# Row LSTM: forget and input gate by one activation over two banks, new values written into moved lanes, each row stored by itself

## What is computed

```python
def _L3_conv_ref(X, W_is, b_is, W_ss, b_ss):
    ...
    its = lax.conv_general_dilated(X, W_is * mask, ..., padding=((0, 0), (1, 1))) + b_is
    def step(carry, row_in):
        h, c = carry
        ss = lax.conv_general_dilated(h, W_ss, ..., padding=((1, 1),)) + b_ss
        g5 = (ss + row_in).reshape(B, 3, 4, Oc, Wd)
        f = jax.nn.sigmoid(g5[:, :, 0].reshape(B, O, Wd))
        i = jax.nn.sigmoid(g5[:, :, 1].reshape(B, O, Wd))
        o = jax.nn.sigmoid(g5[:, :, 2].reshape(B, O, Wd))
        g = jnp.tanh(g5[:, :, 3].reshape(B, O, Wd))
        c_new = f * c + i * g
        h_new = o * jnp.tanh(c_new)
        return ((h_new, c_new), h_new)
    _, hs = lax.scan(step, (h0, c0), xs)      # over the 56 rows
```

## Time and profile before

| | |
|---|---|
| runs | 3912.57, 3913.15, 3914.15 us; median 3913.15 |
| the profiled execution | 3912.36 us, of which the span of the trace is 3910.5 |
| busy over the span | PE 82%, PEld 46%, DVE 70%, ACT 67%, POOL 42% |
| the row LSTM, first matmul to the barrier behind it | 3344.1 to 3718.2 us |

### The profile page before, as it was taken

How to read it: one execution, slowest core, us unless ns; L and a number is a source line. 1 busy time by engine, 2 the same in 40 slices (tenths; PEclk the granted TensorE clock), 3 DMA queues, 4 the chain that set the end, 5 groups by cost and what they waited for, 6 DMA issues and landing times. The chain is left out here.

```text
span 3910.5 us, 70731 instructions
## 1 busy us (share of the span) xinstructions
PE 3205.9 (82%) x20680; PEld 1815.2 (46%) x20680; DVE 2733.1 (70%) x4347; ACT 2623.9 (67%) x4852; POOL 1638.0 (42%) x1502
## 2 busy tenths in 40 slices
PE   5799999978678898999999666878888678677666
PEld 2688888844224343444444222433343334566522
DVE  2566666657319998999999992749999867122256
ACT  4455555559698888989889434966666378465556
POOL 0233333310147888989889761007677600000000
PEclk9899999989889999999999997989999889798988
DMA  4100000012365747576674522210000022400022
GB/s 95 28 14 14 14 14 14 14 32 60 86 165 161 193 134 197 141 209 172 175 204 120 135 58 68 59 36 20 21 21 20 12 50 54 87 13 13 17 56 51
DMA packets 209512, 297.93 MB, mean 76 GB/s; under 512 B 73866, under 2 KB 193854, under 8 KB 208962
## 3 DMA queue, kind: packets, MB, share of 16 engines
q1 hardware_dynamic: 198546, 285.75, 28.2%
q10 hardware_dynamic: 10800, 10.34, 1.1%
HBM read 193.87 MB, written 102.03 MB: 76 GB/s over the span
## 5 line engine op out<-in xcount | busy, mean ns | idle before, releaser
L1586 POOL TENSOR_TENSOR mam_hc<-mam_h,mam_cs 128x896 f32<-128x896 f32 x336 | 704.0, 2096 | 181.4 <-DVE mam_h L1551 93.3
L1551 DVE TENSOR_TENSOR_SCAN mam_h<-mam_a,mam_kept,mam_dbx 128x448 f32<-128x448 f32 x672 | 737.5, 1127 | 19.9 <-ACT mam_a L1437 18.5
L1318 PE MATMUL mam_ps_y<-mam_hc,mam_ident 128*128 128x448 f32 x1344 | 569.7, 557 | 132.5 <-POOL mam_hc L1586 132.2
L1987 POOL TENSOR_TENSOR scan_ch<-scan_h,scan_cs 128x392 f32<-128x392 f32 x256 | 342.6, 1357 | 394.4 <-DVE scan_h L1931 317.3
L1437 ACT ACTIVATE mam_a<-mam_ft,mam_a_neg 128x448 f32<-128x448 f32 x672 | 409.3, 657 | 79.5 <-DVE mam_h L1551 78.7
L1318 PEld LDWEIGHTS mam_ps_y<-mam_hc,mam_ident 128*128 128x128 f32 x1344 | 248.5, 192 | 431.8 <-POOL mam_hc L1586 222.7
L1538 DVE TENSOR_TENSOR mam_dbx<-mam_ps_u,mam_bs 128x448 f32<-128x448 f32 x672 | 380.8, 610 | 34.2 <-DMA mam_bs<-dram_bc 34.2
L766 POOL TENSOR_TENSOR att_prob<-att_prob,att_share 128x588 f32<-128x588 f32 x128 | 151.6, 1184 | 452.5 <-DVE att_share L951 452.5
L2107 PE MATMUL lstm_ps<-lstm_hs,lstm_w_h 64*128 64x224 f32 x1344 | 175.8, 417 | 97.0 <-DVE lstm_hs L2190 97.0
L418 PE MATMUL f_xc_ff<-all_x,f_centre 128*128 (+1 forms) x256 | 127.8, 583 | 138.8 <-DVE all_x L308 138.7
L886 ACT ACTIVATE att_pt<-att_ps_t 128x512 f32<-128x512 f32 x128 | 76.4, 597 | 210.2 <-PE att_ps_t L827 210.2
(11 more groups left out here) (214 smaller groups left out, 7464.4 us busy)
## 6 DMA issues: line engine op xcount, KB each, us to landing
mam_taps<-normed SPq DMA_DIRECT2D x1008, 43.5 KB
mam_bs<-dram_bc SPq DMA_DIRECT2D x28, 896.0 KB, 14.3
mam_cs<-dram_bc SPq DMA_DIRECT2D x28, 896.0 KB, 16.6
mam_ft<-dram_steps SPq DMA_DIRECT2D x42, 448.0 KB, 4.8
normed<-f_staged SPq DMA_DIRECT2D x384, 38.1 KB
f_mixed<-mixed SPq DMA_DIRECT2D x384, 36.8 KB
dram_gs<-mam_gs SPq DMA_DIRECT2D x56, 224.0 KB, 2.1
mam_gt<-dram_gs SPq DMA_DIRECT2D x56, 224.0 KB, 2.7
```

Of the source, the lines that this page charges most:

```text
L1318: mm = pe.matmul(ps_y[p % 2][:, 0:MT], ident[:], hc[t % 2][:, i, :], start=False, stop=(t % 8 == 7 and i == 1))
L1551: dve.tensor_tensor_scan(h[:, n % 8, :], a[t % 3][:, i, :], dbx[:, i, 0:MT], kept[:, at:at + 1], ALU.mult, ALU.add).then_inc(scanned, 1)
L1586: pool.tensor_tensor(hc[t % 2][:], h[:, row:row + 2, :], cs[:, 2 * pair:2 * pair + 2, :], ALU.mult).then_inc(weighed, 1)
L1987: pool.tensor_tensor(out, hd, in_order(cs, 1 - half, d, k), ALU.mult).then_inc(weighed, 1)
```

## The change

- The pairs are made anew: pair 0 is forget and input gate, pair 1 new values and output gate.
- The biases of pair 0 are added on TensorE: one more matmul per half in `from_input`, of `w_bias` (two rows of each half hold the two bias vectors) with a tile of ones. So both gates of both halves go through one Sigmoid without bias, 128 lanes by 2 banks by 224, into `opened`.
- The Tanh of the new values comes behind the second pair's sum; it writes each half into the other half's lanes, so that it lies beside its input gate. Each half counts up `tanhed`.
- The output gate stays two activations, into a tile of its own.
- VectorE's products of forget and input gate are done by halves: kept[half] = opened x cell in the same lanes, as soon as `opened` is there; added[half] = opened x new, read in the other half's lanes and written to this one's, as each Tanh is done. Kept comes before added.
- Each row is stored as it comes, by 4 DMAs of 24 channels by 4 images by 56 values (`store_row`), all on SP but for the last row, of which ScalarE issues two.
- SP loads `w_bias` (64 KB) ahead of the first input rows, and VectorE sets the ones.

```diff
@@ -2009,13 +2009,16 @@
         buf = Buffers(nc, ctx, "lstm")
         w_x = buf.sbuf("w_x", [P, 2, PAIRED, P])
         w_h = buf.sbuf("w_h", [P, 3, PAIRED, P])
-        biases = buf.sbuf("biases", [P, 2, GATES])
-        bias = buf.sbuf("bias", [P, GATES])
+        biases = buf.sbuf("biases", [P, 2, 2])
+        bias = buf.sbuf("bias", [P, 2])
+        w_bias = buf.sbuf("w_bias", [P, P])
+        ones = buf.sbuf("ones", [P, J * SIDE])
         xs = buf.sbuf("xs", [P, J, PAD, PAD])
         hs = buf.sbuf("hs", [P, J, SIDE + 1, PAD])
         cell = buf.sbuf("cell", [P, J, SIDE])
         new = [buf.sbuf(f"new{p}", [P, J, SIDE]) for p in range(2)]
-        gates = [buf.sbuf(f"gates{p}", [P, 3, J, SIDE]) for p in range(2)]
+        opened = [buf.sbuf(f"opened{p}", [P, 2, J, SIDE]) for p in range(2)]
+        output = [buf.sbuf(f"output{p}", [P, J, SIDE]) for p in range(2)]
         kept = [buf.sbuf(f"kept{p}", [P, J, SIDE]) for p in range(2)]
         added = [buf.sbuf(f"added{p}", [P, J, SIDE]) for p in range(2)]
         squashed = [buf.sbuf(f"squashed{p}", [P, J, SIDE]) for p in range(2)]
@@ -2025,12 +2028,12 @@
                                  "zeroed", "stored",
                                  "stored_last"))
         rows_in = [buf.sem(f"rows_in{part}") for part in range(len(LOADED))]
-        summed, tanhed, inputs, forgets, outputs, kepts, addeds, cells, squasheds, hidden = (
-            buf.sem(n) for n in ("summed", "tanhed", "inputs", "forgets", "outputs", "kepts",
-                                 "addeds", "cells", "squasheds", "hidden"))
+        summed, opens, tanhed, outputs, kepts, addeds, cells, squasheds, hidden = (
+            buf.sem(n) for n in ("summed", "opens", "tanhed", "outputs", "kepts", "addeds",
+                                 "cells", "squasheds", "hidden"))
         W = J * SIDE
-        NEW_INPUT, FORGET_OUTPUT = 0, 1
-        FORGET, INPUT, OUTPUT = 0, 1, 2
+        FORGET_INPUT, NEW_OUTPUT = 0, 1
+        NEW, OUTPUT = 0, 1
         LANES = (slice(0, HALF_LANES), slice(HALF_LANES, P))
 
         def each_row(eng, row):
@@ -2059,45 +2062,56 @@
             eng.dma_start(xs[lane + C:lane + 32, J - 1, first:end, :].rearrange(
                 "c y q -> c (y q)"), normed[0, 0:32 - C, at]).then_inc(rows_in[part], 16)
 
-        def store_rows(eng, g, k, done):
-            for j in range(J):
-                eng.dma_start(mixed[k + (j * G + g) * K].rearrange("c (r q) -> c r q", q=SIDE),
-                              group_rows(hs, g)[:, j, bass.ds(k * ROWS + 1, ROWS), 1:SIDE + 1]
-                              ).then_inc(done, 16)
+        by_group = mixed.rearrange("(j g k) c n -> g k c j n", g=G, k=K)
+
+        def store_row(eng, g, k, r, done):
+            eng.dma_start(by_group[g, k][:, :, r * SIDE:(r + 1) * SIDE],
+                          group_rows(hs, g)[:, :, bass.ds(k * ROWS + (r + 1), 1), 1:SIDE + 1
+                                            ].rearrange("c j o q -> c j (o q)")
+                          ).then_inc(done, 16)
 
         with nc.Block() as block:
             @block.sync
             def _(sp):
                 sp.dma_start(w_x[:], w["rl_w_x"]).then_inc(x_weights_in, 16)
+                sp.dma_start(w_bias[:], w["rl_w_bias"]).then_inc(x_weights_in, 16)
                 load_rows(sp, 0)
                 sp.dma_start(biases[:], w["rl_b"]).then_inc(biases_in, 16)
                 load_rows(sp, 1)
                 load_rows(sp, 2)
                 with sp.Fori(0, K - 1) as k:
-                    sp.wait_ge(hidden, k * ROWS + ROWS)
+                    for r in range(ROWS):
+                        sp.wait_ge(hidden, k * ROWS + (r + 1))
+                        for g in range(G):
+                            store_row(sp, g, k, r, stored)
+                for r in range(ROWS - 1):
+                    sp.wait_ge(hidden, (K - 1) * ROWS + r + 1)
                     for g in range(G):
-                        store_rows(sp, g, k, stored)
+                        store_row(sp, g, K - 1, r, stored)
                 sp.wait_ge(hidden, SIDE)
                 for g in range(0, G, 2):
-                    store_rows(sp, g, K - 1, stored_last)
-                sp.wait_ge(stored, 16 * IMAGES * (K - 1))
-                sp.wait_ge(stored_last, 16 * IMAGES)
+                    store_row(sp, g, K - 1, ROWS - 1, stored_last)
+                sp.wait_ge(stored, 16 * G * (SIDE - 1))
+                sp.wait_ge(stored_last, 16 * G)
 
             @block.tensor
             def _(pe):
                 pe.wait_ge(zeroed, 1)
-                pe.wait_ge(x_weights_in, 16)
+                pe.wait_ge(x_weights_in, 32)
                 pe.wait_ge(rows_in[0], 16 * (G + 2))
 
                 def from_input(y, p):
 
                     reached(pe, outputs, y - 1)
+                    for half, lanes in enumerate(LANES):
+                        pe.matmul(ps[p][:, FORGET_INPUT, half, 0:W], w_bias[lanes, :],
+                                  ones[lanes, :], start=True, stop=False)
                     for pair in range(PAIRED):
                         for tap in range(2):
                             for half, lanes in enumerate(LANES):
                                 pe.matmul(ps[p][:, pair, half, 0:W], w_x[lanes, tap, pair, :],
                                           xs[lanes, :, y + 1, tap:tap + SIDE],
-                                          start=(tap == 0), stop=False)
+                                          start=(pair == NEW_OUTPUT and tap == 0), stop=False)
 
                 def row(y, p):
                     reached(pe, hidden, y)
@@ -2128,42 +2142,35 @@
                 def row(y, p):
                     act.wait_ge(summed, y * PAIRED + 1)
                     reached(act, cells, y)
-                    for half, lanes in enumerate(LANES):
-                        act.activation(new[p][lanes].rearrange("c j q -> c (j q)"),
-                                       ps[p][lanes, NEW_INPUT, half, 0:W], ACT.Tanh,
-                                       bias=bias[lanes, 0:1])
-                    for half, lanes in enumerate(LANES):
-                        other = LANES[1 - half]
-                        mm = act.activation(gates[p][lanes, INPUT].rearrange("c j q -> c (j q)"),
-                                            ps[p][other, NEW_INPUT, half, 0:W], ACT.Sigmoid,
-                                            bias=bias[other, 1 + INPUT:2 + INPUT])
-                    mm.then_inc(inputs, 1)
+                    act.activation(opened[p][:].rearrange("c h j q -> c h (j q)"),
+                                   ps[p][:, FORGET_INPUT, :, 0:W], ACT.Sigmoid
+                                   ).then_inc(opens, 1)
                     act.wait_ge(summed, y * PAIRED + 2)
                     reached(act, hidden, y)
                     for half, lanes in enumerate(LANES):
-                        mm = act.activation(gates[p][lanes, FORGET].rearrange("c j q -> c (j q)"),
-                                            ps[p][lanes, FORGET_OUTPUT, half, 0:W], ACT.Sigmoid,
-                                            bias=bias[lanes, 1 + FORGET:2 + FORGET])
-                    mm.then_inc(forgets, 1)
+                        act.activation(new[p][LANES[1 - half]].rearrange("c j q -> c (j q)"),
+                                       ps[p][lanes, NEW_OUTPUT, half, 0:W], ACT.Tanh,
+                                       bias=bias[lanes, NEW:NEW + 1]).then_inc(tanhed, 1)
                     for half, lanes in enumerate(LANES):
                         other = LANES[1 - half]
-                        mm = act.activation(gates[p][lanes, OUTPUT].rearrange("c j q -> c (j q)"),
-                                            ps[p][other, FORGET_OUTPUT, half, 0:W], ACT.Sigmoid,
-                                            bias=bias[other, 1 + OUTPUT:2 + OUTPUT])
-                    mm.then_inc(outputs, 1)
+                        op = act.activation(output[p][lanes].rearrange("c j q -> c (j q)"),
+                                            ps[p][other, NEW_OUTPUT, half, 0:W], ACT.Sigmoid,
+                                            bias=bias[other, OUTPUT:OUTPUT + 1])
+                    op.then_inc(outputs, 1)
                     act.wait_ge(cells, y + 1)
                     act.activation(squashed[p][:], cell[:], ACT.Tanh).then_inc(squasheds, 1)
 
                 each_row(act, row)
                 act.wait_ge(hidden, SIDE)
                 for g in range(1, G, 2):
-                    store_rows(act, g, K - 1, stored_last)
+                    store_row(act, g, K - 1, ROWS - 1, stored_last)
 
             @block.vector
             def _(dve):
 
                 dve.memset(hs[:, :, 0, :], 0.0)
                 dve.memset(hs[:, :, 1:, 0:PAD:PAD - 1], 0.0)
+                dve.memset(ones[:], 1.0)
                 dve.memset(cell[:], 0.0).then_inc(zeroed, 1)
                 dve.wait_ge(biases_in, 16)
                 dve.tensor_tensor(bias[:], biases[:, 0], biases[:, 1], ALU.add
```

(31 more changed lines are left out.)

## The result

| | before | after |
|---|---|---|
| median of the runs | 3913.65 us | 3846.76 us (3842.51 to 3854.38) |
| ratio | | 0.983, 95% interval 0.9815 to 0.9844 |
| the profiled execution, its span | 3912.36, 3910.5 | 3854.38, 3852.5 |

The change makes the kernel 66.9 us faster; the forecast was 3851 with 3843 to 3866. The kernel before was run again beside each set of experiments (medians 3911.7 of 7, 3912.7 of 24, 3913.31 of 15 executions); the ratios of the experiments go by these. One of the 24, 10865.88 us at a clock of 0.485, was in a slow state and stands in no ratio.

A forecast was written before the change was run, and what follows sets the result against it. Bound by one loop per row through three engines, with ScalarE's queue binding and TensorE's low clock a second cost. 3912.36 - 57.1 (rows) + 0.3 (start) - 5.5 (stores) = 3850.1; median 0.8 above, said as 3851; range 3843 to 3866.

The forecast's parts named there:

- Activations: ScalarE in each row: the one 128x448 gate activation takes 0.55 us, gates ready at 2.01, the tanh waits until 2.61.
- Products: VectorE in each row: four half-lane products at 0.392 us each, cell's tanh at 4.44, period 5.43 us instead of 6.13.
- the doubtful row: A profiled 64x392 VectorE operation, 632 ns beside 567 for a whole one, suggesting 0.44 us per half-lane product.
- Halves in other lanes: VectorE, by the skill's rule: a lane switch holds back the next half; priced at 0.10 each, row 5.48 us.
- Clock: TensorE in the rows: idle falls from 2.05 to 0.96 us, no slow rows after the first, 18.6 us gained.
- Start: First row: 0.4 us for the added load, up to 0.8 for more passes, 0.7 given back; together +0.3 us.
- Stores: End of the row LSTM: smaller last stores let the next stage begin earlier, -5.5 us, bounds -3 and -6.
- 3.5 us behind the last hidden product: Sign at the end of the rows: the next stage's first instruction comes 3.5 us behind it instead of 9.5.
- Rival A: TensorE in the rows: about 20 slow rows remain, 1.67 us for a full one, time 3882; chance 0.08 with mixtures.
- Rival B: VectorE's half-lane products cost far more than 0.39 us; at 0.85 each the time is 3931; chance 0.03.
- Rival C: Rows: VectorE's waits and register work, or SP's stores, add 0.15 to 0.2 us each, time 3860; chance 0.11.
- The next stage: Stage behind the row LSTM: work unchanged, 3 us either way allowed for its clock falling otherwise.

The follow-up runs named there:

- after_gates_by_half: The changed kernel with the gates' one activation done as four over half the lanes, without bias: median 3880.28 us.
- after_idler_tensor: The changed kernel without the bias matmuls and the second tap of the input row, 12 passes a row less on TensorE: median 3894.77 us.
- before_busier_tensor: The kernel before with four more matmuls a row, results overwritten, in the part TensorE works ahead: median 3895.35 us, ratio 0.9961.
- after_gates_with_bias: The changed kernel without the bias matmuls, its gates done as four half-lane activations with their biases: median 3922.86 us, ratio 1.0028.

## Why the prediction was right

The forecast took 62.3 us off the three stretches that the change touches (rows 57.1, end 5.5, start -0.3); they are 66.5 us shorter. The 4.2 us between the two are 2.6 in the rows, 1.0 at the end and 0.6 at the start. The median, 3846.8, lies 4.2 below the forecast 3851 too; that the two differences are the same is luck, since single executions of the changed kernel lie up to 12 us apart.

*Activations.* The one of 128x448 from two banks took 545 ns, of 0.55 forecast. The gates are there at 2.01, the tanh starts at 2.61, both as written.

*Products.* Half the lanes were taken at 0.392 like all of them: measured 386 ns, and 385 for those that move values to the other half. The 0.44 of the doubtful row was not needed. The sum gave 4.44 for the cell's tanh; it started at 4.40. The reason is a wrong reading of what comes last: the first output activation starts 0.1 before the second tanh has ended (3566.50 is 0.81 behind 3565.69, and two halves of tanh take 0.91), so the output gates are done at 4.31. VectorE's second added half and the cell bind, not ScalarE's queue. The period was forecast as 5.43 and is 5.39: 2.2 of the 2.6 us by which the rows' gain (57.1 forecast, 59.7 measured) was undersized.

*Halves in other lanes.* The Trainium skill ("VectorE: DVE Perf Modes", Two Vector instructions with no wait between them) would hold the second half back until the first is finished. The rows agree as far as they go: the second kept half starts 0.01 us behind the end of the first. Whether it was held, or would have started there anyway, no run here tells. The price that the prediction put on it, 0.10 for each half, was wrong: two halves take 0.79.

*Clock.* No group was slow, where before 21 were. Two experiments in opposite directions tie the slow rows to TensorE's idle stretch: 1.29 in the kernel before takes them away, 2.06 in the changed kernel brings them back. The weak place of the argument was that the short idle stretches of before all came behind a longer busy one than the new rows have. The changed kernel and after_gates_by_half close it: there 0.93 and 1.53 us of idle time follow busy stretches of 4.46 us row after row, and no group but a first one is slow. Over all traces the groups that were slow, other than a first one, came behind 1.88 to 2.16 us of idle time, and none came behind 1.78 us or less; between the two there is no row. (Where the idle stretch is the same row after row, the longest without slow groups is 1.53; the single ones up to 1.78 each follow a slow group.) Since every edit that changed the idle stretch changed TensorE's share of work in the row with it, the runs do not tell the length of the gap from that share. The Trainium skill ("TensorE: Matmul & The Clock Gate", Why this matters for your kernels) warns only of idle gaps between bursts that are longer than any in these rows; the trace disagrees, with falls behind 1.98 to 2.06 us in the kernel before.

*Start.* The prediction said +0.3, though its terms as written, 0.4 + 0.8 - 0.7, give up to 0.5; measured -0.3. The four more passes of the first row cost 0.75 at the low clock, as forecast (3.87 instead of 3.12 from the first matmul to the first of the hidden row), and the shorter chain gave back 1.0 (4.82 instead of 5.80). The 0.4 for the load of `w_bias` was not seen: the first matmul came 10.4 to 10.8 us behind the first issue in three traces without this load and 10.7 to 11.2 in eight with it and the same rows, 0.2 more in the means, which is less than the traces of either kind differ among themselves. The first group of hidden passes is at full clock:

```profile
3354.78 1.12 PE L2107 MATMUL lstm_ps<-lstm_ones,lstm_w_bias 64*128 64x224 f32 x4 [15.68 <-DMA lstm_xs<-normed]
3355.66 3.23 PE L2112 MATMUL lstm_ps<-lstm_xs,lstm_w_x 64*128 64x224 f32 x16
3358.64 2.57 PE L2121 MATMUL lstm_ps<-lstm_hs,lstm_w_h 64*128 64x224 f32 x24
```

*Stores.* -5.5 forecast, -6.5 measured, outside the bound of -6. (The sign "3.5 us behind the last hidden product" did not follow from the sum, which gives 4.0; it is 2.97.) Two terms were too large. The issue cost was read off a line between 24 and 168 pieces as 0.58; in the rows its median is 0.31, as for 24 pieces, though a row's store has 96, and the last two on a queue took 0.83 together instead of 1.4:

```profile
L2068 SPq DMA_DIRECT2D mixed<-lstm_hs x222: 309/309/4040, 3364.1 to 3660.4; - x111
```

And the next stage began 1.7 us behind the last issue (3662.55 - 3660.83) instead of 2.05. What an issue costs did not go by the pieces. The four issues of a row took SP 1.9 us of the 5.39 in most rows. Some single issues took over 1 us and one 4.04, so that one row's four took 6.1 us, longer than a row; no row was late by it, since nothing in the rows waits for SP.

*Rival A* (the slow clock stays) did not occur in the changed kernel; its price (1.67 for a row slow throughout) is what after_idler_tensor shows. *Rival B*, slower through VectorE's halves, did not occur because a half costs 386 ns; its chain appears where the gates are late. *Rival C*, a row of 5.6, did not occur either: the longest is 5.39.

*The next stage*: 192.2 and 190.0 in the two traces, 188.8 to 193.9 over all; that is movement, and no effect of the change that could be shown.

Of the gain of 66.5 us, then, 18.6 come from the clock, 59.7 - 18.6 = 41.1 from the period, 6.5 from the stores; the 0.3 from the start is less than the traces of the start differ among themselves. Clock and period are counted in this order, the clock first. In the other order the clock's part is larger, since a slow row costs more in the short rows: with 31 of them after_idler_tensor loses 44.5 us. The clock's part is shown by before_busier_tensor, the stores' by the two kernels with exchanged stores, and what makes the row shorter by after_gates_with_bias and after_gates_by_half.

## What to carry to other kernels
In a recurrence through several engines, write one step out instruction by instruction and ask what ends the wait before each; work may be moved or doubled freely where an engine waits for something later (two activations or one, four products or two), and it costs at once where the wait is gone. Look at TensorE's clock in the same rows: an idle stretch of 2 us in a step of 6 cost 18.6 us in 56 steps, and filling part of it with work, even useless work, paid. Adding a bias by a matmul with a tile of ones takes work from the engine that binds and gives it to the one that idles, and here it also helps to keep the clock up.
